# One order of work for VectorE in a chunked recurrence: halves interleaved, first state products of the next chunk ahead of the second own terms

## What is computed

```python
def step(S, inp):
    qi, ki, vi, ei = inp
    kh = jnp.einsum('bchd,bhde->bche', ki, S)
    target = vi - ki
    mu = jnp.mean(kh, -1, keepdims=True)
    rstd = jax.lax.rsqrt(jnp.var(kh, -1, keepdims=True) + EPS)
    kh_hat = (kh - mu) * rstd
    g = w * kh_hat + b - target
    gw = g * w
    v_new = (gw - jnp.mean(gw, -1, keepdims=True) - kh_hat * jnp.mean(gw * kh_hat, -1, keepdims=True)) * rstd
    A = jnp.einsum('bchd,bshd->bhcs', qi, ki)
    A = jnp.where(tri, A, 0.0) * jnp.transpose(ei, (0, 2, 1))[:, :, None, :]
    qh = jnp.einsum('bchd,bhde->bche', qi, S) - jnp.einsum('bhcs,bshe->bche', A, v_new)
    o = qi + _ln(qh, w, b)
    S = S - jnp.einsum('bchd,bche->bhde', ki * ei[..., None], v_new)
    return (S, o)
```

## Time and profile before

| what | value |
|---|---|
| time, median of 3 executions | 396.2 us |
| lowest and highest | 395.01 and 397.21 us |
| the profiled execution, first to last instruction | 394.5 us |
| TensorE matmul busy | 350.8 us (89%) |
| VectorE busy | 260.5 us (66%) |
| ScalarE busy | 190.8 us (48%) |
| GpSimd busy | 107.4 us (27%) |
| mean granted TensorE clock | 0.969 |

### The profile page before, as it was taken

The page is one execution under the profiler, slowest core; times in us unless marked ns, Lnnn a source line. Parts: engine busy times, 40 slices in busy tenths (PEclk is TensorE's granted clock), DMA queues, the critical chain, the costliest instruction groups (busy, mean ns, idle before and its releaser), DMA issues.

```text
span 394.5 us, 11644 instructions
## 1 busy us (share of the span) xinstructions
PE 350.8 (89%) x5106; PEld 243.8 (62%) x5110; DVE 260.5 (66%) x519; ACT 190.8 (48%) x356; POOL 107.4 (27%) x117
## 2 busy tenths in 40 slices
PE   3899997978879769699899999999999999999993
PEld 3343674534535433398688797887977879784641
DVE  0487965279899998775444574855758547386564
ACT  3042795543554425244625555555565555744320
POOL 3007296720000000000053251522615217053001
PEclk9999996999989968989999999999999999999999
DMA  8994000000220300139020010100102000000000
GB/s 249 251 325 150 2 2 4 5 3 5 72 94 5 112 2 2 22 107 208 7 56 0 27 30 15 55 0 16 55 14 55 2 15 0 15 2 0 15 1 27
DMA packets 17633, 19.99 MB, mean 51 GB/s; under 512 B 3360, under 2 KB 15024, under 8 KB 17328
## 3 DMA queue, kind: packets, MB, share of 16 engines
q1 hardware_dynamic: 17552, 19.24, 18.0%
q10 hardware_dynamic: 32, 0.02, 0.0%
HBM read 18.07 MB, written 1.18 MB: 49 GB/s over the span
## 4 chain that ended last, share of the span: by engine, by line
PE 64%; DVE 19%; ACT 7%; issue 4%; POOL 2%; DMA 1%; SPq 1%; POOLq 0%; DVEq 0%; ACTq 0%
PE ps L649 15%; PE ps L715 12%; PE ps L463 6%; PE ps L707 4%; PE ps L555 4%; PE ps L692 4%; PE ps L734 3%; PE ps L665 2%; PE ps L574 2%; PE ps L592 2%; PE ps L759 2%; DMA wg<-in_L_attn_Wg_dram 1%; PE ps L683 1%; PE ps L752 1%; PE ps L674 1%
## 5 line engine op out<-in xcount | busy, mean ns | idle before, releaser
L649 PEld LDWEIGHTS ps<-x1t,xwq 128*128 128x128 f32 x512 | 60.9, 196 | 7.8 <-issue 4.9
L649 PE MATMUL ps<-x1t,xwq 128*128 128x128 f32 x512 | 63.7, 283 | 1.8 <-ACT x1t L1055 1.8
L715 PE MATMUL ps<-mvo,cxp 128*128 128x256 f32 x256 | 58.2, 382 | 0.4 <-DVE gs L1477 0.4
L1605 POOL TENSOR_SCALAR rstd<-mv 128x1 f32<-128x1 f32 x22 | 4.8, 218 | 176.6 <-DVE mv L1419 176.6
L715 PEld LDWEIGHTS ps<-mvo,cxp 128*128 128x128 f32 x256 | 47.6, 190 | 6.6 <-issue 0.7
L555 PE MATMUL ps<-ctxt,xwk 128*128 128x512 f32 x64 | 39.9, 739 | 0.0
L1019 ACT ACTIVATE qt<-ps 128x512 f32<-128x512 f32 x32 | 19.1, 597 | 36.0 <-PE ps L649 36.0
L939 ACT ACTIVATE ksq<-ps 128x512 f32<-128x512 f32 x32 | 19.0, 593 | 30.0 <-PE ps L555 21.1
L941 ACT ACTIVATE kt<-ps,gks 128x512 f32<-128x512 f32 x32 | 21.9, 683 | 0.0
L1428 DVE TENSOR_SCALAR x<-rr,mv,rstd 128x256 f32<-128x256 f32 x16 | 6.6, 413 | 22.5 <-POOL rstd L1606 22.5
L1026 ACT ACTIVATE qsq<-ps 128x512 f32<-128x512 f32 x32 | 19.0, 593 | 4.7 <-PE ps L665 4.6
(11 more groups left out here) (224 smaller groups left out, 680.2 us busy)
## 6 DMA issues: line engine op xcount, KB each, us to landing
rkb<-kscale SPq DMA_DIRECT2D x16, 256.0 KB, 4.0
xn<-in_x_dram SPq DMA_DIRECT2D x4, 512.0 KB, 5.8
ctx<-in_ctx_dram SPq DMA_DIRECT2D x4, 512.0 KB, 8.2
xwo<-in_L_xattn_Wo_dram SPq DMA_DIRECT2D x1, 2048.0 KB, 14.1
xwq<-in_L_xattn_Wq_dram SPq DMA_DIRECT2D x4, 512.0 KB, 4.7
w1n<-in_L_ffn_w_gate_up_dram SPq DMA_DIRECT2D x1, 1408.0 KB, 8.9
xwv<-in_L_xattn_Wv_dram SPq DMA_DIRECT2D x1, 1024.0 KB, 11.8
xwk<-in_L_xattn_Wk_dram SPq DMA_DIRECT2D x1, 1024.0 KB, 16.3
```

Of the source, the lines that this page charges most:

```text
L649: last = mm(bank(n % 2, P, t * P), xwq[qn][:, k * BANK + t * P:k * BANK + (t + 1) * P], x1t[:, (i % 2) * D + k * P:(i % 2) * D + (k + 1) * ...
L715: last = mm(bank(6 + turn_of[("y", i, 0)] % 2, D), cxp[:, h * P:(h + 1) * P], mvo[:, h * D:(h + 1) * D], start=h == 0, stop=h == XH - 1)
```

## The change

VectorE no longer finishes one half before the other: each step is a function of its own that returns its number (`mark`), and `need(n)` waits for a number only where its result is read. Between two steps of one half stand steps of the other half, of the output stage and of the state update. The read of qhR and the update of the state for half 1 move into the next chunk. In chunk 0 both halves' chains run ahead of a_masked(0). TensorE does state_products(c + 1, 0) ahead of own_terms(c, 1), with other places for the key units; ScalarE's order follows, with keys(6) ahead of the first state_root. KEY_PLACES goes. The instructions themselves stay, apart from `mean_square`, which nobody called.

```diff
@@ TensorE
-            for c in range(NCH):
-                places = iter(KEY_PLACES[c])
-                if c >= 1:
-                    state_products(c, 0)
-                    keys(next(places))
-                    state_products(c, 1)
-                keys(next(places))
-                if c < NCH - 1:
-                    scores_ttt(c + 1, 0)
-                    keys(next(places))
+            keys(1)
+            own_terms(0, 0)
+            keys(2)
+            scores_ttt(1, 0)
+            keys(1)
+            state_products(1, 0)
+            own_terms(0, 1)
+            keys(1)
+            scores_ttt(1, 1)
+            keys(1)
+            for c in range(1, NCH - 1):
+                keys(2)
+                state_products(c, 1)
+                keys(1)
+                scores_ttt(c + 1, 0)
+                keys(1)
+                scores_ttt(c + 1, 1)
+                keys(2)
                 own_terms(c, 0)
-                if c < NCH - 1:
-                    keys(next(places))
-                    scores_ttt(c + 1, 1)
-                keys(next(places))
+                keys(2)
+                state_products(c + 1, 0)
+                keys(1)
                 own_terms(c, 1)
-                for n in places:
-                    keys(n)
+            keys(2)
+            state_products(NCH - 1, 1)
+            keys(4)
+            own_terms(NCH - 1, 0)
+            keys(1)
+            own_terms(NCH - 1, 1)
+            keys(1)
             key_unit(next(units))
@@ ScalarE
-            for c in range(NCH):
-                places = KEY_PLACES[c]
...
-            output_root(2 * NCH - 2)
+            k_blocks(1)
+            keys(6)
+            for c in range(1, NCH):
                 state_root(c, 0)
+                keys(2)
                 output_square(c - 1)
                 if c < NCH - 1:
                     k_blocks(c + 1)
+                    keys(1)
+                    state_root(c, 1)
+                    output_root(2 * c - 1)
+                    keys(4)
+                    gated_square(c - 1)
+                    keys(1)
+                    output_root(2 * c)
+                    keys(1)
+                else:
+                    keys(2)
+                    state_root(c, 1)
+                    output_root(2 * c - 1)
+                    keys(2)
+                    gated_square(c - 1)
+                    keys(1)
+                    output_root(2 * c)
+                    keys(1)
             last_root(0)
@@ VectorE
+            def mark(ins):
                 steps[0] += 1
                 ins.then_inc(sem("dve_step"), 1)
-                dve.wait_ge(sem("dve_step"), steps[0])
+                return steps[0]
+
+            def need(n):
+                dve.wait_ge(sem("dve_step"), n)
...
+            def first_chunk():
+                kb_rows(0)
+                dve.wait_ge(sem("kv_rows"), 1)
+                dve.wait_ge(sem("p_rows"), 1)
...
+                d0 = centred(0, 0, p_of(0, 0))
+                size = [mark(V.tensor_scalar(half(rn, h, B), ne_of(0, h), TTT_EPS ** -0.5, None, ALU.mult)) for h in range(2)]
+                need(sums1)
+                d1 = centred(0, 1, p_of(0, 1))
...
+                u0 = u_rows(0)
+                need(d1)
+                u1 = u_rows(1)
...
+                u_blocks(0, 0)
+                u_blocks(0, 1)
+                a_masked(0)
+                qh_rows(0, 0)
+                state_turned(0, 0)
+
+            def chunk(c):
+                last = c == NCH - 1
+                kh0 = kh_rows(c, 0)
...
+                    out_turned(c - 2)
+                qh_rows(c - 1, 1)
+                turned1 = state_turned(c - 1, 1)
+                r0 = kh_inverse(c, 0)
...
+                kh1 = kh_rows(c, 1)
+                need(gx_product0)
+                sums0 = both_sums(0)
+                need(kh1)
+                sq1 = kh_square(1)
+                need(sums0)
+                d0 = centred(c, 0, gw_of(0))
+                need(sq1)
+                kh_sums(1)
+                ax0 = along_x(0)
+                output_sums(2 * c - 1)
+                need(ax0)
+                need(d0)
+                e0 = across_x(0)
+                r1 = kh_inverse(c, 1)
+                need(e0)
+                need(size0)
+                u0 = u_rows(0)
+                need(r1)
+                hat1 = x_hat(1)
+                need(u0)
+                u_swap(0)
+                need(hat1)
+                scaled1 = gw_scaled(1)
+                u_blocks(c, 0)
+                normal = output_inverse(2 * c - 1)
...
+                sums1 = both_sums(1)
+                need(gated)
+                out_biased(c - 1)
+                need(sums1)
+                d1 = centred(c, 1, gw_of(1))
+                qh_rows(c, 0)
+                ax1 = along_x(1)
+                if not last:
+                    turned0 = state_turned(c, 0)
...
+                    state_added(c, 0)
+                need(e1)
+                need(size1)
+                u1 = u_rows(1)
+                output_sums(2 * c)
+                need(u1)
+                u_swap(1)
+                u_blocks(c, 1)
+
+            first_chunk()
+            for c in range(1, NCH):
+                chunk(c)
+            inverse = output_inverse(2 * NCH - 2)
+            qh_rows(NCH - 1, 1)
...
             last_square(qhR, 0)
-            output_sums(2 * NCH - 2)
+            need(inverse)
+            scaled = out_scaled()
             last_scale(qhR, 0)
             last_gate(0)
             last_square(sup, 1)
-            output_inverse(2 * NCH - 2)
-            out_c(NCH - 2)
+            need(scaled)
+            out_turned(NCH - 2)
```

More of the change, by code:

```diff
@@ new lines, in kh_inverse, with x_hat, gw_scaled, gw_shifted @@
+            def kh_inverse(c, h):
+                dve.wait_ge(sem("sd_ready"), 2 * (c - 1) + h + 1)
+                return mark(V.reciprocal(half(rs, h, B), half(sdc, h, B)))
+            def x_hat(h):
+                return mark(V.tensor_tensor(groups(half(xh, h), DH), groups(half(khR, h), DH), spread(half(rs, h, B), B, DH), ALU.mult))
+            def gw_scaled(h):
+                return mark(V.tensor_tensor(groups(gw_of(h), 32), groups(half(xh, h), 32), half_feature(w2R, h), ALU.mult))
+            def gw_shifted(c, h):
+                dve.wait_ge(sem("p_rows"), c + 1)
+                return mark(V.tensor_tensor(gw_of(h), gw_of(h), p_of(c, h), ALU.add))
@@ new lines, in along_x, with across_x, u_rows @@
+            def along_x(h):
+                return mark(V.tensor_tensor(groups(gx_of(h), DH), groups(half(xh, h), DH), spread(m2_of(h), B, DH), ALU.mult))
+            def across_x(h):
+                return mark(V.scalar_tensor_tensor(out=half(dd, h), in0=gx_of(h), scalar=-1.0 / DH, in1=half(dd, h),
+                                                   op0=ALU.mult, op1=ALU.add))
+            def u_rows(h):
+                return mark(V.tensor_tensor(groups(half(uR, h), DH), groups(half(dd, h), DH), spread(half(rn, h, B), B, DH), ALU.mult))
@@ new lines, in u_swap, with ub_part, u_blocks @@
+            def u_swap(h):
+                V.stream_shuffle(half(us_, h), half(uR, h), [(n + C) % 32 for n in range(32)]).then_inc(sem("u_swapped"), 1)
+            def ub_part(h, m, odd):
+                o = half(ub, h, CW).rearrange("p (m o h e) -> p o h m e", o=2, h=2, e=DH)[:, odd, m]
+                src = half(uR if m == odd else us_, h).rearrange("p (m h e) -> p h m e", h=2, e=DH)[:, m]
+                V.tensor_scalar(o, src, mask_of(m), None, ALU.mult).then_inc(sem("ub_ready"), 1)
+            def u_blocks(c, h):
@@ L1347, in _ @@
                 kb_rows(c)
+                need(hat0)
+                scaled0 = gw_scaled(0)
                 a_masked(c)
[L1349 to L1359 removed]
@@ new lines, in chunk @@
+                need(normed)
+                gated = out_gated(c - 1)
+                need(gx_product1)
+                sums1 = both_sums(1)
[7 more added lines that the diff above has]
+                    turned0 = state_turned(c, 0)
+                need(ax1)
+                need(d1)
+                e1 = across_x(1)
@@ L1367, in last_square @@
+                if not last:
+                    need(turned0)
+                    state_added(c, 0)
[3 more added lines that the diff above has]
+                output_sums(2 * c)
+                need(u1)
+                u_swap(1)
+                u_blocks(c, 1)
[4 more added lines that the diff above has]
+            qh_rows(NCH - 1, 1)
             def last_square(src, n):
```

191 lines of the change are left out of this document (88 added, 103 removed).

## The result

The changed kernel takes 402.6 us (median of 4 runs, 400.2 to 404.0), the one before 396.7 (4 runs, 395.0 to 397.3) in the same comparison: ratio 1.0168, 95% interval 1.0131 to 1.0204. It is slower by about 6 us where 1.6 us of gain was forecast. A few executions came out over 1.5% above the fastest of their kernel, and the ratios leave them out, so a ratio can differ a little from that of the medians. The profiled execution of the changed kernel took 400.2 us, the fastest of its four, with a span of 398.7, against a span of 394.5 before. The traces thus show 4.2 us of the difference.

A forecast was written before the change was run, and what follows sets the result against it. TensorE's instruction supply was taken to pace chunk 1, VectorE chunks 2 and 3. The walk's gain of 161.9 - 159.1 = 2.8 us, less 1.2, left 1.6: 396.2 - 1.6 = 394.6 us, range 391.2 to 399.8.

The forecast's parts named there:

- VectorE's term: VectorE, each chunk: independent instructions start 0.34 us apart instead of 0.46, so a chunk takes 21.4 us instead of 25.9.
- The blocks: TensorE's instruction supply: one 16 KB packet per 256 instructions, so a pause every 128 matmuls, 3.73 us each.
- walk: Step-by-step timing of the recurrence at fixed prices: last transposition at 159.1 in the new order, 161.9 in the old.
- The new waits: VectorE waits for the root of chunk 1 (about 5 us), own_terms(1,0) (3.1) and own_terms(2,0) (3.8).
- The slow block: TensorE's instruction block crossed during the loads after mg_done 4: priced at 9.4 us after mg_done 4, resuming at 118.3.
- What I take off: Deduction from the 2.8 us gain: 0.9 for TensorE's clock in chunk 3, 0.3 for loads of og_ready 2; 1.6 left.
- I take the six alone: Start of chunk 0: GpSimd holds six VectorE instructions but not the eight ub parts; own_terms(0,0) start at 66.1.
- rival 4: First chunk late: ub parts wait for GpSimd too, own_terms(0,0) at 69.2, each us goes through; 397.4 us, chance 0.09.
- The case of my own: Main forecast for the whole kernel: 394.6 us, its own range 392.7 to 396.9, chance 0.50.
- the block behind the weights: Block crossed in own_terms(1,1) falls behind mg_done 4's loads, coming 9.5 us after it instead of 3.3; 399.6, chance 0.13.
- the waits for nothing: Waits cost nothing on VectorE, 0.46 for every instruction; the walk ends 8 us later, 402 to 403, chance 0.05.
- rivals 1 and 2: First: chunk 0's blocks ready sooner, 393.5 or 392.5, chance 0.13. Second: instruction supply no limit, 382, chance 0.10.

The follow-up runs named there:

- best version: Changed kernel with GpSimd's rows held back, first state root behind four key units, SyncE's loads behind mg_done 6, 18 small matmuls ahead of own_terms(3,1): 390.7 us, ratio 0.9876.

## Why the prediction was wrong

**The steps that held.** VectorE's term: 0.33 against 0.46, 21.1 us of solid work in chunk 2 (21.4), and 9 us more with the waits back (8). The blocks: still 128 matmuls apart, 3.84 us in the rows shown, and two blocks less save 8 us (how much of it by the blocks alone is open). The walk's rule "at least 3.73 after the one before" was too strict: already in the kernel before, the seven blocks are 3.45 to 4.10 apart, and only their mean is 3.73. The new waits, each with its releaser: 5.9 for the root of chunk 1 (5), covered; 1.9 and 6.2 for own_terms(1,0) and (2,0) (3.1 and 3.8). The slow block: forecast 9.4 us after own_terms(1,1), resumed at 122.48, which is 9.3 after their end at 113.2. The warm matmuls and the main loop cost nothing.

**The step that failed: "What I take off".** It put the clock at 0.9, in chunk 3 alone, and the loads at 0.3 more. The runs: covering the pause at the start is worth 3.9, moving the loads 4.4 (the slow block, which the walk had in it, included), both together 7.4. The walk's prices (half batch 1.2, key unit 0.95) were all of 2.4 GHz, and TensorE ran 37 of 108 us at 1.2 GHz. I had made the new pauses myself and read their lengths off the walk, but only as waits. The low clock behind them makes every key unit and half batch dearer just where TensorE, not VectorE, sets the end. It shows from the first block on: the resumption at 77.28 was at 73.9 in the walk, 3.4 sooner, of which the late start is 2.0, and the rest came where own_terms(0,0) took 2.78 and four key matmuls 2.87. Nor was it unseen: own_terms at 1.80 are such a row, and I used it at one place only. The slow block's distance was right; what stands behind it was not: the first pause of 2.46 was followed by four keys at 3.66 and by own_terms(2,0) at 131.8, where the walk had the block at 126.2.

**The second failed step: "I take the six alone".** Two of the four pairs of ub parts are held as well, 1.4 and 1.0 us longer than the 0.47 of a free pair. That was rival 4 (chance 0.09), and it came out at 68.1, between its 69.2 and my 66.1. Whether its price was 1.0 per us, as I had it, isn't settled: on its own an earlier start brought 0.7 us by the ratios and 1.2 in the trace for 3.2 (1.0168 to 1.0150), with new pauses in other places, and the interval is wider than the difference.

**The numbers on the path.** Walk, changed kernel, both losses taken out, and the best version, each read from its trace:

| | walk | changed | pause covered, loads later | best version |
|---|---|---|---|---|
| own_terms(0,0) start | 66.1 | 68.1 | 68.2 | 64.0 |
| own_terms(1,1) end | 108.8 | 113.2 | 111.8 | 109.0 |
| chunk 3 starts | 131.3 | 137.9 | 133.6 | 130.7 |
| own_terms(3,1) start | 152.1 | 158.3 | 153.7 | 150.7 |
| last transposition ends | 159.1 | 166.8 | 162.3 | 157.6 |

With both losses out the kernel stays 1.6 to 3.0 behind the walk up to own_terms(3,1), 2.1 of which it brings from the start, and loses 1.6 more in the tail to the clock there: 8.6 us from own_terms(3,1) on where the walk had 7.0. The best version runs the tail at 2.4 GHz and takes 6.9. That version comes near the walk, but it isn't the walk's kernel: its loads are moved, so it lacks the slow block that the walk paid for, and it starts 2 us sooner. That the walk would be right for a TensorE that never slows isn't shown; no run has such a one (means of 0.88 and 0.92 in these two).

**The chances.** The case of my own had 0.50, and its mechanism did happen. The range ended at 399.8 because no rival had the clock as its mechanism. The slower side held only the late first chunk, the block behind the weights and the waits for nothing. Within the chances there is a slip of 0.02: rivals 1 and 2 have 0.23 together, not 0.21. The last transposition is 7.7 behind the walk (166.8 against 159.1): 2.0 of it at the start, 1.5 in the tail, and 4.2 between 68 and 158 us, where the low clock and the loads overlap. The forecast had allowed for 2.1 of the 7.7 (0.9 that the walk missed in the old kernel too, and the 1.2 taken off). How much of that middle part is the clock alone and how much the pause of 2.46 that the loads lengthened was not taken apart: no run changed the one without the other there.

## What to carry to other kernels

A reordering that makes TensorE wait in new places has two prices: the wait, and everything that follows at half the clock. Price the work behind each new pause (here 3.83 and 2.46 us, once 1.05) by the rows at 1.2 GHz, and try small matmuls in the pause if it can't be removed. An earlier step is worth what the next pauses leave of it: on its own it may bring nothing that can be measured.

## What was not expected of the hardware

- **Adding nine matmuls made the kernel 3.9 us faster.** TensorE is the engine that sets the pace there, and 2.81 us of useless work on it paid more than it cost, since it stood where TensorE had been idle for 3.83.
- **GpSimd holds VectorE up to the end of its own instruction.** Each held instruction ended 0.1 to 0.4 us behind one of GpSimd's. Beside GpSimd, d took 0.94 and 1.49 (0.42 alone), the two step sizes on 16 columns 1.31, and two ub parts of 128 columns 1.83 (0.47 alone). The kernel before gave the mirror image: chain instructions at 1.38 in place of 0.42 once GpSimd's work was moved beside them, and 1.26% (5 us) on the total. Not held in the same stretch were the sums (0.37 and 0.40) and the shuffles (0.44).
- **Instructions cost where the products hardly take time.** A half batch of scores takes 1.19 us with 64 matmuls and 1.26 with 128, and yet 256 matmuls and as many weight loads less saved 8 us.
